# A gated cross-attention and mixture-of-experts layer in fp32: the busiest expert's matrix products, each split into two column tiles of 64 tokens

## The reference, cut to what matters

```python
x = x + tanh(g_xattn) * (0.6 * sigmoid(si + sj + b) + 0.4 * layernorm(x))     # 4 x 256 tokens of 256
xf = layernorm(x).reshape(1024, 256)
scores = sigmoid(xf @ w_router)                     # 32 experts, in 8 groups of 4
# the best 4 groups, in them the best 6 experts of each token:
combine[token, expert] = scores where chosen, else 0
g = einsum('th,ehm->etm', xf, gate_w)               # H = 256, M = 176
u = einsum('th,ehm->etm', xf, up_w)
eo = einsum('etm,emh->eth', silu(g) * u, down_w)
routed = einsum('te,eth->th', combine, eo)
shared = silu(xf @ sh_gate_w) * (xf @ sh_up_w) @ sh_down_w
x = x + tanh(g_ffn) * (routed + shared)
```

## Time and profile before

| | |
|---|---|
| median of 3 runs | 262.04 us (261.15 to 264.52) |
| the profiled execution | 263.16 us, of which the span of the trace is 261.3 us |
| TensorE matmul busy | 221.7 us, 85% of the span |
| TensorE weight loads busy | 172.3 us, 66% |
| GpSimd, VectorE, ScalarE busy | 157.4, 129.9, 79.6 us |
| mean granted TensorE clock | 0.921 of full speed |
| share of TensorE in the chain that ended last | 62% |

### The profile page before, as it was taken

One profiled execution on the slowest core, in us unless ns is written; L12 is line 12 of the kernel. 1 busy time (PEld: TensorE's weight loads), 2 busy tenths in 40 slices (PEclk: granted clock), 3 DMA queues, 4 the chain that ended last, 5 costly groups with the idle time before them and its releaser, 6 DMA issues.

```text
span 261.3 us, 5099 instructions
## 1 busy us (share of the span) xinstructions
PE 221.7 (85%) x1043; PEld 172.3 (66%) x1044; DVE 129.9 (50%) x528; ACT 79.6 (30%) x222; POOL 157.4 (60%) x188
## 2 busy tenths in 40 slices
PE   7994987895699978799999999999999999999000
PEld 6893775683477745477777777777877777677000
DVE  2898685949634523234344443444434434344434
ACT  3534121111011121333434344434444344333100
POOL 6352867787787873446565665575656656465510
PEclk9686799999589999799999999999999999999655
DMA  6999999999999569899765675966766767354978
GB/s 198 268 303 315 406 402 358 321 292 358 309 316 369 183 174 314 242 230 220 156 118 110 106 128 99 161 110 108 120 98 119 115 103 123 42 61 48 215 234 269
DMA packets 41018, 53.70 MB, mean 206 GB/s; under 512 B 5135, under 2 KB 35439, under 8 KB 40999
## 3 DMA queue, kind: packets, MB, share of 16 engines
q1 hardware_dynamic: 24944, 30.40, 39.3%
q0 software_dynamic: 11280, 18.36, 35.4%
q10 hardware_dynamic: 4774, 4.74, 6.9%
HBM read 31.72 MB, written 21.77 MB: 205 GB/s over the span
## 4 chain that ended last, share of the span: by engine, by line
PE 62%; DVE 17%; DMA 9%; issue 4%; another core or an unknown queue 3%; ACT 1%; POOL 1%; ACTq 0%; SPq 0%; POOLq 0%
PE pG L738 25%; PE pY L752 17%; PE pX L732 5%; PE pH L746 4%; DMA sum_dram<-xnT,idx 4%; PE pG L761 4%; PE pY L780 3%; DMA xg<-rows_dram 2%; PE pG L677 2%; PE pY L688 2%; DMA wgu<-sum_dram 2%; DMA wij<-in_L_xattn_W_dram 2%; DVE wgu L1006 1%; DVE rows L898 1%
## 5 line engine op out<-in xcount | busy, mean ns | idle before, releaser
L439 POOL DMA_INDIRECT sum_dram<-xnT,idx x56 | 87.0, 1553 | 61.5 <-ACT xnT L553 35.6
L738 PE MATMUL pG<-wgu,sdown 128*128 x224 | 76.7, 465 | 2.0 <-issue 1.8
L426 POOL DMA_INDIRECT rows_dram<-rows,row_i x48 | 47.2, 983 | 18.7 <-issue 11.1
L752 PE MATMUL pY<-wd,sup 88*128 x224 | 58.4, 384 | 0.0
L1126 DVE COPY sup<-pH 88x256 f32<-88x256 f32 x56 | 23.6, 421 | 62.2 <-PE pH L746 57.3
L738 PEld LDWEIGHTS pG<-wgu,sdown 128*128 128x128 f32 x224 | 38.5, 191 | 15.1 <-issue 3.0
L553 ACT ACTIVATE xnT<-pY,wt 128x256 f32<-128x256 f32 x56 | 26.5, 473 | 57.5 <-issue 20.2
L752 PEld LDWEIGHTS pY<-wd,sup 88*128 88x128 f32 x224 | 38.6, 192 | 3.4 <-issue 0.2
L746 PEld LDWEIGHTS pH<-ident,sgate 128*88 128x88 f32 x112 | 17.9, 162 | 17.1 <-DVE sgate L1122 3.9
L546 ACT ACTIVATE sgate<-pG 128x176 f32<-128x176 f32 x56 | 17.8, 317 | 29.5 <-PE pG L738 27.4
L746 PE MATMUL pH<-ident,sgate 128*88 128x128 f32 x112 | 21.9, 277 | 2.5 <-DVE sgate L1122 2.5
(11 more groups left out here) (183 smaller groups left out, 244.5 us busy)
## 6 DMA issues: line engine op xcount, KB each, us to landing
wgu<-in_L_ffn_gate_w_dram SPq DMA_DIRECT2D x8, 704.0 KB, 9.2
wgu<-in_L_ffn_up_w_dram SPq DMA_DIRECT2D x8, 704.0 KB, 11.6
wd<-in_L_ffn_down_w_dram SPq DMA_DIRECT2D x8, 640.0 KB
sum_dram<-zeros POOLq DMA_DIRECT2D x3, 1152.0 KB
wgu<-sum_dram SPq DMA_DIRECT2D x12, 256.0 KB, 4.0
rows<-rows_dram ACTq DMA_DIRECT2D x16, 144.5 KB
xg<-rows_dram ACTq DMA_DIRECT2D x16, 144.5 KB
rows_dram<-zeros SPq DMA_DIRECT2D x8, 289.0 KB, 4.2
```

The source lines that it names most:

```text
L426: pool.indirect_dma_start(rows_dram[:, :], bass.IndirectOffsetOnAxis(ap=row_i[:, j, k:k + 1], axis=0), lines[:, j * ROW:j * ROW + LINE], N ...
L439: pool.indirect_dma_start(sums_dram[into[s]][:, :], bass.IndirectOffsetOnAxis(ap=idx[:, s:s + 1], axis=0), y[s], None, compute_op=ALU.add) ...
L738: ins = nc.tensor.matmul(pG[par][:, 0:2 * M].rearrange("t (g m) -> t g m", g=2), xT[:, par, k, :], wgu[:, bass.ds(e, 1), :, k, :].rearrang ...
L752: ins = nc.tensor.matmul(pY[par][:, 0:H], hT[0:MI, par, i, :], wd[:, bass.ds(e, 1), i, :], start=(i == 0), stop=(i == I - 1))
```

## The change

In the dense stage alone, each product is issued twice: once with tokens 0 to 63 of the block as the stationary operand and its result on PSUM partitions 0 to 63, once with tokens 64 to 127 and partitions 64 to 127. Both stream the same columns. `tile_position` names the half of the array's columns that holds the operand. The steps of ScalarE and VectorE, the transposes, the semaphores and the data are as before; the semaphore is incremented by the last of the products.

```diff
     FLOW = 3
+    SIDES = [slice(0, P // 2), slice(P // 2, P)]
...
             def gate_up_busy(j):
                 for k in range(K):
-                    ins = nc.tensor.matmul(pG[j % 2][:, 0:2 * M].rearrange("t (g m) -> t g m", g=2),
-                                           xnT[:, k, j * P:(j + 1) * P], busy_gu[:, :, k, :],
-                                           start=(k == 0), stop=(k == K - 1))
+                    for ts in SIDES:
+                        ins = nc.tensor.matmul(pG[j % 2][ts, 0:2 * M].rearrange("t (g m) -> t g m", g=2),
+                                               xnT[:, k, j * P + ts.start:j * P + ts.stop], busy_gu[:, :, k, :],
+                                               start=(k == 0), stop=(k == K - 1), tile_position=(0, ts.start))
                 ins.then_inc(s_bgu, 1)
...
                 for i in range(I):
-                    ins = nc.tensor.matmul(pY[j % 2][:, 0:H], hT[0:MI, j % 2, i, :], busy_d[:, i, :],
-                                           start=(i == 0), stop=(i == I - 1))
+                    for ts in SIDES:
+                        ins = nc.tensor.matmul(pY[j % 2][ts, 0:H], hT[0:MI, j % 2, i, ts], busy_d[:, i, :],
+                                               start=(i == 0), stop=(i == I - 1), tile_position=(0, ts.start))
                 ins.then_inc(s_by, 1)
```

## The result

The changed kernel takes 272.95 us (median of 4 runs, 272.4 to 273.55) against 262.54 us for the kernel before (median of 4 runs), a ratio of 1.039 with a 95% interval of 1.032 to 1.046. It is slower by 10.4 us, where 5 us had been forecast.

The account below looks back on a forecast made before the run. TensorE's stream of passes was taken to bound the dense stage. Unpartnered passes 2.7 plus handovers 3.2, less 1.0 taken back, gave 4.9, say 5 us: 262.04 + 5 = 267.0 us, range 263.5 to 278.5 us.

Parts of the forecast that it names:

- What bounds the kernel before: Dense stage: bound by TensorE's stream of passes alone, 18.91 us busy, so a later stage end reaches the kernel's end.
- The columns that stream set the price of a pass: Dense products: a pass costs its streamed columns, about 1180 a us, however many tokens are stationary.
- the exclusion of a gain: Dense stage: 2n passes over at most two halves take n slots at least, so no gain.
- The lower bound: Split products: one pass without partner at the end of each of 10 runs, 2.7 us added.
- the handover: Split products: the upper half's load waits for the lower pass 2 to start, 54 x 0.06 = 3.2 us added.
- Switching: Dense stage: 20 switches between halves and whole array, taken to cost nothing.
- the rival: Dense stage: overlap, and a drain at each of 20 switches, 0.16 us each, 3.2 us on top: 270.2 us; chance 0.05.
- the sign that the prediction named: Dense stage: a drain would start L771's first transpose more than 0.1 us later than the end of the stream.
- free handovers: Split products, rival: the upper half's load is pulled ahead while idle, 2.7 us added, less 1: 263.8 us; chance 0.15.
- Nothing in them is added to the path: Dense stage: the other engines' steps and the semaphores add nothing to the path.
- The takeback: TensorE's gap behind the dense stage: a quicker tile load gives back 1 us, bounds nothing and 4.7 us.
- The chances: Whole kernel: slower by over 2% 0.56, within 2% 0.42, faster by over 2% 0.02.

Follow-up runs that it names:

- e1: Only the gate and up products split, down products whole as in the kernel before; 259.96 us, ratio 1.011 to the kernel before.
- e2: Only the down products split, gate and up products whole as in the kernel before; 259.72 us, ratio 1.010 to the kernel before.
- e4: The change with only tokens 0 to 63 of each block computed, on the lower half of the array; 261.80 us, ratio 1.020 to the kernel before.
- e13: The same lower-half kernel as e4, on another chip; 266.35 us, ratio 1.012 to the kernel before.
- e10: The same kernel as e3 (whole array, streamed columns split in two), on another chip; 276.78 us, ratio 1.044 to the kernel before.
- e12: The kernel before, unchanged, traced on the chip of e10; 269.04 us.
- e14: The change, unaltered, on the chip of e13; 273.69 us, ratio 1.036 to the kernel before.
- e5: The kernel before, unchanged, traced on the chip of e6; 264.39 us.
- e16: The kernel before, unchanged, traced on the chip of e13 and e14; 265.95 us.
- e3: Kernel before with each dense product's streamed columns split in two, tokens whole, 36 loads and matmuls a block; 260.05 us, ratio 0.999 to the kernel before.
- e6: The change, unaltered, on another chip than the first measurement; 273.59 us, ratio 1.034 to the kernel before.
- e8: The change with each block's second transpose moved behind the down product, 15 split stretches instead of 10; 269.67 us, ratio 1.019 to the kernel before.
- e9: The change, unaltered, on the chip of e10; 278.38 us, ratio 1.041 to the kernel before.
- e7: The change with the transposes made as plain products split over the halves, 48 instructions a block; 275.91 us, ratio 1.045 to the kernel before.
- set 2: The runs e5 to e8 on one chip, with their own runs of the kernel before (median 264.74 us).
- set 3: Four runs on one chip, e9, e10, e12 and a gate and up split alone, with their own runs of the kernel before (median 265.11 us).
- set 1: The runs e1 to e4 on one chip, with their own runs of the kernel before (median 257.14 us).

## Why the prediction was wrong

**What bounds the kernel before: right.** The stage's length went to the end almost in full: tile 0's gate and up product starts 8.8 us later than before (101.38 against 92.59), the steady tiles run 7.4 us later.

**The columns that stream set the price of a pass: right**, and so was the exclusion of a gain.

**The lower bound and the handover: wrong in substance.** The working let an upper pass run only beside the lower half's second pass, because records of matmuls start in program order, and so counted 2.7 us for unpartnered passes and 3.2 us for handovers. Both measured nothing: eight passes take 1.19 us as four did, which leaves no room for a pass without a partner, so the upper half's first pass must run beside the lower half's first. Of the two rules of the Trainium skill that the prediction weighed, the one on packing (TensorE: Matmul & The Clock Gate, Measured speedup vs the span model), that a further tile adds almost nothing, is what the chain shows.

**Switching: wrong, and it had been a rival.** "I take nothing for it" rested on the earlier trace rows, matmuls of 64 columns behind whole-array ones early in the program. They could not show a switch: the kernel before names no `tile_position` anywhere, and these are narrow operands on the undivided array. In the stage a stretch costs 0.31 us, 0.16 for each of 20 switches, which is exactly the rival's own price. The rule of the Trainium skill (TensorEngine Tiling (Array Packing), Key Properties) that a change of mode drains TensorE agrees with the cost in this trace and in e1, e2, e4 and e13. That the cost is a drain is not shown: the sign that the prediction named, a first transpose more than 0.1 us behind the end of the stream, did not come. By the records the transposes at 78.51 start 0.06 us before the gate and up product ends (77.17 + 1.40); before, it was 0.16 us (77.62 against 76.43 + 1.35). The rival's other half, the handovers, did not come, so its 270.2 us was too high as a sum for what it named. Paid switches and free handovers, 262.04 + 3.1 - 1.0 = 264.1 us, was the combination to forecast from these terms; its stage, 2.8 to 3.1 us longer, is what e4 and e13 show on two chips. The prediction had 5.9 us for the stage, but none of them came by the mechanism that they were put down to, so that a forecast of half the loss is no half success.

**"Nothing in them is added to the path": the step that failed most.** The prediction looked at the durations of the other engines and not at how they learn of TensorE's progress. On the chip of the first measurement the increments fell behind by about 1.1 us a block, and this, with the low clock after the idle times, cost 5.2 of the stage's 8.3 us. The trace of before held a hint that the prediction passed over: at the end of the stage SyncE and VectorE both move at 94.58 and 94.60 on the last down product, which ends at 92.76 by its record, and a silu comes at 96.08 for products that end at 93.94.

```profile
92.33 0.38 ACT L541 ACTIVATE sdown<-pX 128x256 f32<-128x256 f32 x1 [0.26 <-PE pX L732]
...
94.00 1.35 PE L738 MATMUL pG<-wgu,sdown 128*128 x4
...
94.58 0.78 SPq L303 DMA_DIRECT2D wd<-in_L_ffn_down_w_dram  x2
94.60 0.48 DVE L1150 SCALAR_TENSOR_TENSOR xs<-pY,busy_w,xs 128x256 f32<-128x256 f32 x1 [2.58 <-remote]
...
96.08 0.32 ACT L546 ACTIVATE sgate<-pG 128x176 f32<-128x176 f32 x1 [3.37 <-PE pG L738]
...
96.85 0.39 ACT L541 ACTIVATE sdown<-pX 128x256 f32<-128x256 f32 x1 [0.45 <-remote]
...
99.00 0.32 ACT L546 ACTIVATE sgate<-pG 128x176 f32<-128x176 f32 x1 [1.77 <-remote]
```

That the lateness comes with the number of instructions is shown on other chips (e10 beside e12, e14 beside e13); on the first chip itself it was not tested.

**The takeback: right in size.** 1.0 us was taken; tile 0 is 8.8 us late, tile 12 only 7.4 (136.65 against 129.30). The tile load in the gap was not quicker, though: 7.04 us instead of 5.80. What TensorE regained there is less waiting between the first tiles, so the reason given was wrong. Part of the gap of the kernel before is itself late reports: the products of tile 1, at 94.00, end at 95.35, and their silu starts at 99.00. After the change the silu of tile 0 starts on time, at 104.13 for products that end at 104.09 (101.44 + 2.65), against 2.1 us late before.

```profile
101.44 2.65 PE pG L739 x4
...
104.13 0.32 ACT L547 ACTIVATE sgate<-pG 128x176 f32<-128x176 f32 x1 [4.17 <-PE pG L739]
```

**The rest of the 10 us.** From the start of the last tile's gate and up product to the end of the span it is 25.8 us where it was 23.6. The traces of the sixteen experiments, which all have the same tail, give 23.3 to 26.8 us, and the kernel before alone 24.6 to 26.0 (e5, e12, e16), so these 2.2 us are not charged to the change. Another 0.7 us lies outside the span, 2.6 us instead of 1.9; it stays unexplained. In the other kernels with 36 instructions a block (e3, e6, e8, e9, e10 and e14) 2.3 to 3.0 us lie outside it as well, in e7, with 48, 1.9.

The chances had 0.56 on slower by over 2%, and that came (the single ones that are listed add up to 1.02, a slip). The number was half of what was measured, since a term that was not on the list, late reports with the low clock behind them, is at 5.2 us larger than any term that the sum had.

## What to carry to other kernels

Splitting a product whose stationary operand fills the array had nothing to gain here: its two halves together took 1.19 us, as the whole did, and every passage between split and whole-array work cost about 0.16 us. (Narrow operands, where there may be a gain, were not run.) Count the instructions too: with 36 loads and matmuls a block instead of 20 and the same time of streaming, the increments that others wait for came microseconds late in every trace of the change. With the halves left out (e3 and e10) they did so on one of two chips. To see that, compare the start of the waiting engine with the end of the record that it waits for, block by block; busy shares and the records themselves look healthy.

## What the runs showed that I had not expected

- **Late reports by TensorE come at a pace of their own, but not at one rate.** In the change on the first chip and in set 2, 36 loads and matmuls a block gave silus 3.7 us apart, 0.10 us an instruction, while the transfer engines were full (share 1.01 from 78 to 88 us); behind 89 us, with a share of 0.33, they were 2.95 us apart, 0.08 us. In set 3 it was 0.125 us. In set 1, no report was late in any of four traces, 36 instructions in 2.3 us among them. And in the kernel before on the first chip, the reports of 28 loads and matmuls behind the dense stage took from 92.33 to 99.00 us, 0.24 us each, so the number of instructions alone doesn't give the lateness.

```profile
78.00:88.00 10.00, 10.00 (x72) 5.00 (x70) 3.11 (x9) 0.95 (x3) 8.05 (x15) 1.00 1.01 345
88.00:98.00 10.00, 6.55 (x46) 3.03 (x42) 4.20 (x11) 0.95 (x3) 8.19 (x14) 0.97 0.33 123
```

- **What makes them late stays open.** The late traces name "remote" as the releaser of many of these waits, 8.6 us of ScalarE's in e6 and none in e3, which is taken here to mean that the releasing increment is missing from the trace. That the recording of the trace itself takes part would fit this; no run tests it, since every time here comes from an execution that was recorded. Full transfer engines alone don't explain it: e3 had a share of 1.03 in its whole stage and nothing late, and in the kernel before reports fell 1.8 us behind between 90 and 94 us, at shares of 0.22 and 0.41.

- **The two halves start together although the program names two lower passes ahead of the first upper one**, and a whole-array product next to a split one costs about as much as a transpose next to it (0.14 us in e1, 0.19 in e2, against 0.14 and 0.17).
